# Softmax sums of pairs of key blocks: GpSimd adds the exponentials ahead of TensorE's ones matmuls, with four buffers of exponentials

## What is computed

```python
def _L0_attn_ref(x, q_w, k_w, v_w, q_b, k_b, v_b, out_w, out_b):
    ...
    attn = jnp.einsum('bhqd,bhkd->bhqk', q, k) * scaling
    probs = jax.nn.softmax(attn, axis=-1)
    out = jnp.einsum('bhqk,bhkd->bhqd', probs, v)
    out = out.transpose(0, 2, 1, 3).reshape(B, S, D)
    return out @ out_w.T + out_b
...
x = x + _L0_attn_ref(_layernorm(x, axis=-1), L0_attn_q_w, L0_attn_k_w, L0_attn_v_w, L0_attn_q_b, L0_attn_k_b, L0_attn_v_b, L0_attn_out_w, L0_attn_out_b)
```

## Time and profile before

| | |
|---|---|
| median of 3 runs | 1898.21 us (1896.54 to 1898.46) |
| the profiled execution | 1895.96 us |
| its span, first to last instruction | 1894.0 us, 28397 instructions |
| TensorE busy | 1565.4 us, 83% |
| VectorE busy | 1178.8 us, 62% |
| ScalarE busy | 864.6 us, 46% |
| GpSimd busy | 495.0 us, 26% |
| mean granted TensorE clock | 0.933 of full speed |

### The profile page before, as it was taken

The page is one execution under the profiler, slowest core; times in us unless marked ns, Lnnn a source line. Parts: engine busy times, 40 slices in busy tenths (PEclk is TensorE's granted clock), DMA queues, the critical chain, the costliest instruction groups (busy, mean ns, idle before and its releaser), DMA issues.

```text
span 1894.0 us, 28397 instructions
## 1 busy us (share of the span) xinstructions
PE 1565.4 (83%) x9300; PEld 608.4 (32%) x9301; DVE 1178.8 (62%) x1722; ACT 864.6 (46%) x1045; POOL 495.0 (26%) x417
## 2 busy tenths in 40 slices
PE   1899999999949863677779999999949999989827
PEld 1323323233226641333322323333223232323213
DVE  3664756647545535999756463646543676767678
ACT  1353352533523323777545445454635555463612
POOL 1503315033120014311131221212123141414117
PEclk9999999999979986888889999999979999999968
DMA  3700202102033445100031020202212020303002
GB/s 111 247 21 23 67 0 64 25 22 67 24 109 130 148 111 117 23 1 0 1 89 34 12 55 0 67 0 67 89 67 67 24 67 0 89 0 87 1 28 89
DMA packets 80844, 106.08 MB, mean 56 GB/s; under 512 B 14113, under 2 KB 51361, under 8 KB 80673
## 3 DMA queue, kind: packets, MB, share of 16 engines
q1 hardware_dynamic: 77216, 97.14, 17.3%
q0 software_dynamic: 3584, 8.39, 2.1%
HBM read 49.26 MB, written 18.35 MB: 36 GB/s over the span
## 4 chain that ended last, share of the span: by engine, by line
PE 59%; issue 15%; DVE 15%; ACT 4%; POOL 3%; DMA 2%; SPq 1%; DVEq 0%; POOLq 0%; ACTq 0%
PE ps L398 28%; PE ps L716 15%; PE ps L803 6%; PE ps L664 3%; PE ps L688 2%; ACT arena L914 2%; DVE arena L1630 1%; DVE xn L186 1%; PE ps L1517 1%; DVE arena L1098 1%; SPq L623 1%; DVE stats L175 1%; PE ps L737 1%; DVE arena L1641 1%; DVE arena L969 1%
## 5 line engine op out<-in xcount | busy, mean ns | idle before, releaser
L914 ACT ACTIVATE arena<-ps 128x1024 f32<-128x1024 f32 x384 | 372.1, 1024 | 175.9 <-PE ps L803 175.3
L716 PE MATMUL ps<-arena 128*32 128x512 f32 x3072 | 391.5, 616 | 32.8 <-DVE arena L969 24.0
L935 DVE TENSOR_REDUCE arena<-ps 128x2 f32<-128x1024 f32 x256 | 306.4, 1220 | 154.6 <-PE ps L664 154.5
L398 PE MATMUL ps<-xt,w 128*128 128x512 f16 (+1 forms) x1872 | 298.8, 312 | 32.6 <-DVE arena L1003 20.6
L803 PE MATMUL ps<-arena 97*128 97x512 f16 (+1 forms) x768 | 207.6, 383 | 9.7 <-ACT arena L914 6.0
L398 PEld LDWEIGHTS ps<-xt,w 128*128 128x128 f16 (+1 forms) x1872 | 155.0, 100 | 170.8 <-issue 67.1
L398 PE MATMUL ps<-w,arena 128*128 128x512 f16 (+1 forms) x804 | 178.7, 379 | 12.7 <-issue 12.7
L1204 POOL TENSOR_TENSOR arena<-arena 128x512 f16<-128x512 f32 x96 | 115.1, 1201 | 244.1 <-ACT arena L900 206.1
L896 ACT ACTIVATE arena<-ps,arena 128x512 f32<-128x512 f32 x96 | 65.8, 686 | 222.2 <-PE ps L398 179.4
L1115 POOL TENSOR_TENSOR arena<-arena 128x512 f32<-128x512 f32 x36 | 50.5, 1404 | 378.0 <-DVE arena L974 378.0
L1098 DVE TENSOR_SCALAR arena<-arena 128x1024 f32<-128x1024 f32 x128 | 106.7, 839 | 67.1 <-ACT arena L914 66.4
(11 more groups left out here) (176 smaller groups left out, 1909.8 us busy)
## 6 DMA issues: line engine op xcount, KB each, us to landing
arena<-arena SPq DMA_DIRECT2D x576, 64.0 KB, 2.0
raw<-in_ctxT SPq DMA_DIRECT2D x8, 1024.0 KB, 5.4
raw<-in_ffn_parts SPq DMA_DIRECT2D x16, 512.0 KB, 3.5
sorted_x<-arena SPq DMA_DIRECT2D x1, 4864.0 KB, 25.3
arena<-sorted_x SPq DMA_DIRECT2D x19, 256.0 KB, 3.5
sorted_y<-arena SPq DMA_DIRECT2D x19, 256.0 KB, 2.1
out<-x SPq DMA_DIRECT2D x16, 256.0 KB, 2.1
x<-in_x SPq DMA_DIRECT2D x1, 3072.0 KB, 13.8
```

The lines of the kernel that those rows point to most:

```text
L398: last = pe.matmul(out, left[l](cl[k]), right[r](cr[k]), start=start and k == 0 and a == 0, stop=stop and k == n - 1 and a == 2)
L716: last = pe.matmul(self.m.ps[HD * j:HD * (j + 1), 7 if ones else 6, :], left, self.pt[:, u % 2, j * S:(j + 1) * S], start=kb == 0, stop=kb ...
L914: act.activation(self.pt[:, u % 2, 2 * h * S:(2 * h + 2) * S], flat(self.m.ps[:, 2 * h:2 * h + 2, :]), ACT.Exp, scale=SOFTMAX_SCALE).then_ ...
L935: v.tensor_reduce(self.mx[:, g % 2, j:j + 2, t:t + 1].rearrange("p h t -> p (h t)"), self.slot_banks(item, b), AX.X, ALU.max).then_inc(sel ...
```

## The change

In the two self-attentions GpSimd adds the exponentials of two units, 2n and 2n+1, into one buffer, in four instructions of 128x512 (`pool_pair`). That is done for n = 0 to 6; TensorE then multiplies the sum of the pair by ones, instead of each unit, and units 14 and 15 are multiplied by ones as before. A group's two pairs are read by TensorE at the end of steps 4g+3 and 4g+5 (`sums_at`), those of group 3 in step 15 and behind it. There is one buffer for the pair's sum, so GpSimd waits until TensorE has read the pair before. There are four buffers of exponentials: the two of `pt` and the two of `raw`, in which weights lie while they are loaded; so the following phase's first weights are loaded only after the last sums.

VectorE inverts a group's sums one unit later, in step 4g+6, writes the inverse to bank 7 and does the multiplication that GpSimd did (`dve_context`). The norm is applied after unit 11 instead of 12. The values' matmuls no longer wait for the turn of the sums, in the cross-attention neither: there the ones matmuls do.

```diff
-        self.pt = take(2 * HG * S).rearrange("p (n t) -> p n t", n=2)
-        self.vb, self.vhigh = self.pt[:, 1, 0:D], self.pt[:, 1, D:2 * D].bitcast(F16)[:, 0:D]
+        pt = take(2 * HG * S).rearrange("p (n t) -> p n t", n=2)
+        self.vb, self.vhigh = pt[:, 1, 0:D], pt[:, 1, D:2 * D].bitcast(F16)[:, 0:D]
+        self.pts = [pt[:, 0], pt[:, 1]] if cross else [pt[:, 0], pt[:, 1], flat(m.raw[:, 0]), flat(m.raw[:, 1])]
+        if not cross:
+            self.pair_sum = turning if rope else flat(m.tails[1])
...
-        self.pv_done, self.ctx_free = s("pv_done", NB * NH), s("ctx_copied", NB * (C - 1))
+        self.values_done, self.unit_summed, self.ctx_free = s("values_done", NB * NH), s("unit_summed", NB * (NH if cross else 2)), s("ctx_copied", NB * (C - 1))
+        self.paired, self.pair_read = (s(name, 0 if cross else NB * self.ADDS * n) for name, n in (("pairs_added", HG), ("pair_sums_read", 1)))
...
         if self.rope:
+        if not self.cross:
+            sp.wait_ge(*self.at(self.unit_summed, NB * 2))
...
+    def pe_values(self, pe, u, b):
         g, kb = divmod(u, T)
-        if not ones:
-            for h in range(2):
-                pe.wait_ge(*self.at((self.clipped if self.cross else self.exp_done)[h], b * NH + u + 1))
-            if kb == 0 and g:
-                pe.wait_ge(*self.at(self.ctx_free, b * (C - 1) + g))
-                pe.wait_ge(*self.at(self.sums_read, b * C + g))
-            if u == 0:
-                pe.wait_ge(*self.at(self.normed, b * C))
-                if not self.cross:
-                    pe.wait_ge(*self.at(self.slot_free[1], self.slot_count(1, b + 1)))
+        for h in range(2):
+            pe.wait_ge(*self.at((self.clipped if self.cross else self.exp_done)[h], b * NH + u + 1))
+        if kb == 0 and g:
+            pe.wait_ge(*self.at(self.ctx_free, b * (C - 1) + g))
+        if u == 0:
+            pe.wait_ge(*self.at(self.normed, b * C))
+            if not self.cross:
+                pe.wait_ge(*self.at(self.slot_free[1], self.slot_count(1, b + 1)))
         for j in range(HG):
-            left = self.ones if ones else self.v[:, kb, HD * (HG * g + j):HD * (HG * g + j + 1)]
-            last = pe.matmul(self.m.ps[HD * j:HD * (j + 1), 7 if ones else 6, :], left,
-                             self.pt[:, u % 2, j * S:(j + 1) * S], start=kb == 0, stop=kb == T - 1,
-                             tile_position=(0, HD * j))
-        if ones:
-            last.then_inc(self.pv_done, 1)
+            last = pe.matmul(self.m.ps[HD * j:HD * (j + 1), 6, :], self.v[:, kb, HD * (HG * g + j):HD * (HG * g + j + 1)],
+                             self.p(u)[:, j * S:(j + 1) * S], start=kb == 0, stop=kb == T - 1, tile_position=(0, HD * j))
+        last.then_inc(self.values_done, 1)
+    def p(self, u):
+        return self.pts[u % len(self.pts)]
+    def sums_at(self, u):
+        if self.cross:
+            return [((u - 1) // T, ("unit", u - 1), u % T == 1, u % T == 0)] if u else []
+        found = []
+        if u < NH and u % T == T - 1:
+            found.append((u // T, ("pair", u // 2 - 1), True, False))
+        if u < NH and u > T and u % T == 1:
+            found.append((u // T - 1, ("pair", (u - T) // 2 + 1), False, True))
+        if u >= NH - 1:
+            found.append((C - 1, ("unit", u - 1), False, u == NH))
+        return found
+    def pe_sums(self, pe, u, b):
+        for g, (kind, n), first, done in self.sums_at(u):
+            if first and g:
+                pe.wait_ge(*self.at(self.sums_read if self.cross else self.normed, b * C + g))
+            if kind == "pair":
+                pe.wait_ge(*self.at(self.paired, HG * (b * self.ADDS + n + 1)))
+            p = self.pair_sum if kind == "pair" else self.p(n)
+            for j in range(HG):
+                last = pe.matmul(self.m.ps[HD * j:HD * (j + 1), 7, :], self.ones, p[:, j * S:(j + 1) * S],
+                                 start=first, stop=done, tile_position=(0, HD * j))
+            if kind == "pair":
+                last.then_inc(self.pair_read, 1)
+            else:
+                last.then_inc(self.unit_summed, 1)
     def pe_proj(self, pe, n, b):
         m = self.m
...
             if u:
-                self.pe_values(pe, u - 1, b, ones=False)
+                self.pe_values(pe, u - 1, b)
             self.pe_planned(pe, b, u, 3)
-            if u:
-                self.pe_values(pe, u - 1, b, ones=True)
+            self.pe_sums(pe, u, b)
         for i in range(T):
             self.wait_read(pe, ("v", i), b)
...
             for u in range(NH):
                 g, kb = divmod(u, T)
                 for h in range(2):
                     act.wait_ge(*self.at(self.st_full[h], b * NH + u + 1))
-                    act.wait_ge(*self.at(self.pv_done, b * NH + max(u - 1, 0)))
-                    act.activation(self.pt[:, u % 2, 2 * h * S:(2 * h + 2) * S], flat(self.m.ps[:, 2 * h:2 * h + 2, :]),
+                    before = u - len(self.pts)
+                    act.wait_ge(*self.at(self.values_done, b * NH + max(before + 1, 0)))
+                    if self.cross:
+                        act.wait_ge(*self.at(self.unit_summed, b * NH + max(before + 1, 0)))
+                    elif before >= 0:
+                        act.wait_ge(*self.at(self.paired, HG * (b * self.ADDS + before // 2 + 1)))
+                    act.activation(self.p(u)[:, 2 * h * S:(2 * h + 2) * S], flat(self.m.ps[:, 2 * h:2 * h + 2, :]),
...
-    def dve_invert(self, v, g, b):
-        v.wait_ge(*self.at(self.pv_done, b * NH + T * (g + 1)))
+    def dve_invert(self, v, g, b, out=None):
+        if self.cross:
+            v.wait_ge(*self.at(self.unit_summed, b * NH + T * (g + 1)))
+        elif g < C - 1:
+            v.wait_ge(*self.at(self.pair_read, b * self.ADDS + 2 * g + 2))
+        else:
+            v.wait_ge(*self.at(self.unit_summed, b * 2 + 2))
         v.wait_ge(*self.at(self.normed, b * C + g))
         v.transpose(self.sums, self.m.ps[:, 7, :]).then_inc(self.sums_read, 1)
         v.wait_ge(*self.at(self.sums_read, b * C + g + 1))
         one = self.inverse.rearrange("p (n k) -> p n k", k=1)
         v.reciprocal(one, blocked(self.sums)[:, :, 0:1]).then_inc(self.reciprocals, 1)
         v.wait_ge(*self.at(self.reciprocals, b * C + g + 1))
-        v.transpose(blocked(self.sums), one.broadcast_to([P, NQ, HD])).then_inc(self.inverted, 1)
+        v.transpose(blocked(self.sums if out is None else out), one.broadcast_to([P, NQ, HD])).then_inc(self.inverted, 1)
+    def dve_context(self, v, g, b):
+        v.wait_ge(*self.at(self.inverted, b * C + g + 1))
+        v.wait_ge(*self.at(self.ctx_free, b * (C - 1) + g + 1))
+        v.tensor_tensor(self.ctxn, self.ctxn, self.m.ps[:, 7, :], ALU.mult).then_inc(self.normed, 1)
...
-            if g and kb == 1:
-                self.dve_invert(v, g - 1, b)
+            if g and kb == (1 if self.cross else 2):
+                self.dve_invert(v, g - 1, b, None if self.cross else m.ps[:, 7, :])
+                if not self.cross:
+                    self.dve_context(v, g - 1, b)
...
-            if u == 12 and not self.cross:
+            if u == 11 and not self.cross:
                 if self.rope:
...
+        self.pool_context_low(g, c, b)
+
+    def pool_context_low(self, g, c, b):
         g.wait_ge(*self.at(self.ch, b * C + c + 1))
         g.tensor_tensor(self.ct[:, 1, c, :], self.ctxn, self.ct[:, 0, c, :], ALU.subtract).then_inc(self.cl, 1)
+
+    def pool_pair(self, g, n, b):
+        for h in range(2):
+            g.wait_ge(*self.at(self.exp_done[h], b * NH + 2 * n + 2))
+        if n == 0:
+            g.wait_ge(*self.at(self.fl, (b + 1) * self.NPROJ))
+        g.wait_ge(*self.at(self.pair_read, b * self.ADDS + n))
+        for j in range(HG):
+            cols = slice(j * S, (j + 1) * S)
+            g.tensor_tensor(self.pair_sum[:, cols], self.p(2 * n)[:, cols], self.p(2 * n + 1)[:, cols], ALU.add).then_inc(self.paired, 1)
...
-        for c in range(C - 1):
-            if c == C - 2:
+        for n in range(self.ADDS):
+            if n == self.ADDS - 2:
                 self.norm.pool(g, b)
-            self.pool_context(g, c, b)
+            self.pool_pair(g, n, b)
+            if n > 1 and n % 2 == 0:
+                self.pool_context_low(g, n // 2 - 1, b)
```

18 lines of the change are left out of this document (11 added, 7 removed).

## The result

| | before | after |
|---|---|---|
| median of three runs | 1898.21 us | 1928.08 us (1924.8 to 1936.2) |
| profiled execution | 1895.96 us | 1936.2 us (span 1934.4) |
| after / before | | 1.017, 95% interval 1.013 to 1.021 |

What follows compares the result with a forecast made beforehand. TensorE, busy 83%, was taken as the bound, VectorE's reductions pacing steps with p's. attn1 +12.8, attn0 +13.6, clock +5.6 and xattn -3.7 gave +28.3 on 1895.96, 1924.3; forecast 1925, range 1898 to 1942.

Steps and rivals of the forecast that it cites:

- All four signs: Idle before pair 3/4 products; norm instructions 1.4 us; step 6's second p waits; output projection 21.7 us after unit 11.
- Tail and norm: Unit 11 to output projection: norm meets pair 5's additions, x 5.8 us after the power; about +2.6 us a batch.
- rival 3: More falls of the clock, from waits at step 6, pair 3, unit 12's scores and x: 1936; chance 0.13.
- Front: First exponentials to unit 11's: unit 11 starts 0.6 us later a batch in attn1, 0.8 in attn0.
- The walk: Step-by-step timeline of attn1 batch 2 and attn0 batch 1, from the first exponentials to unit 11.
- the second p of step 6: In attn1 batch 2 it waits behind the inversion until t = 22.75, where before it stood at 21.2.
- GpSimd's loop: Additions, product and crossings: 6.3 us for two units, against 5.64 in steps without p, 6.6 to 6.9 mid-batch.
- 1.2 us of waiting at pair 3: In attn1 batch 2 TensorE reaches pair 3 at t = 31.3; GpSimd's additions end at 32.4.
- Rival 1: GpSimd stays hidden, the inversion fits ahead of the reductions and the middle runs at 6.3 us: 1883; chance 0.14.
- The clock: One fall to the lower clock per attn0 batch behind the wait for x, 1.4 us each; none in attn1.
- Cross-attention: Step 13's values no longer wait for the sums; VectorE's clipping is the next wait: -0.9 us a batch.
- The turn of the sums in step 13: In the self-attentions it no longer holds the values (1.54 us), but lies ahead of the same wait: no gain.

Runs made afterwards that it cites:

- e6_small_adds: The changed kernel with each GpSimd addition over 8 of its 512 columns, a pair's ones matmul reading its first block: 1897.0 us.
- e7_half_reductions: The changed kernel with each VectorE reduction of the maxima over 256 of its 512 columns per bank: 1894.7 us.
- e8: The changed kernel with both additions of 8 columns and reductions over half their columns: 1850.0 us.
- e10_three: The changed kernel with moments and power earlier, inversion and context behind the step's last reduction, and two pair-sum buffers in the attention without rotation: 1900.4 us.
- e1_split: The kernel before with only the wait for the turn of the sums moved from values to ones matmuls, separate semaphores, no pairs: 1870.2 us.
- e9_before_half_reductions: The kernel before with each reduction of the maxima over 256 of its 512 columns per bank: 1886.7 us, against 1895.8 beside it.

## Why the prediction held, and where it did not

**Outcome.** Right in sign and size: 1928.1 for 1925, inside the range. All four signs that it named for being right are in the rows. But its steps fared unevenly, and that the sum came so near is in part luck: the fronts lost 17.2 us in the profiled execution where it had 5.6, the cross-attention gave 9.1 where it had 3.7.

**Tail and norm: right, with a second wait beside it in `attn1`.** x 5.9 us behind the power (forecast 5.8), tails +2.6 and +4.05 with the clock (2.6 and 4.0). In `attn0` e6_small_adds shows it by removal: without additions beside the norm the tail falls by 5.4 us. In `attn1` it falls by 0.5 us only: there the maxima's DMA ahead of unit 12, with the fall of the clock that came behind it, costs nearly as much once x is no longer late. The sum left that wait out (rival 3 names the scores of unit 12). It did no harm to the forecast, since x was awaited behind it.

**Front: the mechanism was one of two, and the other was larger.** The walk had the p's and the second p of step 6 in it (forecast t = 22.75, measured 1272.06 - 1249.94 = 22.1), but the text put the loss on GpSimd's loop, "nearly the pace of before in the middle", and expected 1.2 us of waiting at pair 3, where the row has 0.47. For the two batches that it walked through it gave +0.6 and +0.8, where +0.8 (`attn1` batch 2) and +4.5 (`attn0` batch 1) were measured. The fronts of e6 and e7 show what holds them: of 320.5 us in after, e6_small_adds takes away 10.9 and e7_half_reductions 36.7. The loop is one limit there, VectorE's reductions are the larger one. The loop's sizes (4.97 us of additions, 6.2 us from pair 3's start at 1277.60 to pair 4's at 1283.80) were right to 0.1 us. What was missed is a sentence: the ones matmuls were what TensorE did while VectorE reduced. The prediction saw that "steps with two p's ... hold idle time already" and used it only for steps 1 and 2. Rival 1, with GpSimd hidden and the inversion fitting in, was priced at 1883; e6_small_adds, where the additions are as good as gone and the reductions stay, is at 1897.0.

**The clock: right in kind, far too small.** Forecast 5.6 us, only behind the wait for x in `attn0`. The matmuls of after take 40 us more in the eight heads than the same matmuls in e8, whose clock is 0.97 to 1.00 against 0.87 to 0.97. Falls came in steps 1 to 4 of `attn0` too, behind waits of 1.14 and 1.33 us, and in `attn1` behind 1.74. One of them:

```profile
225.01 0.28 PE L688 MATMUL ps<-ident,arena 128*16 128x128 f32 x1 [1.14 <-DVE arena L978]
...
226.22 1.94 PE L723 MATMUL ps<-arena 128*32 128x512 f32 x8
```

The row that could have told this was there: in the kernel before the same step showed a fall in three of four batches. In after step 1 fell in three batches again, and steps 2 and 3 now with it. What that costs can be read in e10_three: steps 2 and 3 last 4.0 and 3.7 us in its batch of 60.2 us, 5.4 and 5.3 in those of 63.5.

**Cross-attention: mis-sized.** -0.9 forecast per batch, -2.3 measured. The next wait is the clipping, as the prediction said, 1.40 us long. What it left out is that the shorter wait also spares the fall of the clock (3.40 us for a row that takes 1.92 at full clock).

**The turn of the sums in step 13 "gives nothing" in the self-attentions.** So in after, where x is awaited right behind it. Without pairs it gives 1.6 to 1.7 us a batch (e1_split).

**Not foreseen, and not the change's: the end.** Behind the last heads, in code that is the same, the profiled run of after lost 5.9 us. VectorE's four int32 instructions there (1.42 us for four at that place before) met GpSimd's:

```profile
1910.16 5.46 DVE L1886 TENSOR_SCALAR arena<-arena 128x512 int32<-128x512 int32 x4
1915.55 1.42 DVE L1889 TENSOR_SCALAR arena<-arena 128x512 f32<-128x512 f32 x4
```

The stretch behind the last heads is 93.4 to 93.7 us long in seven of the fourteen profiled runs and 98.9 to 99.6 in the other seven, e9_before_half_reductions among these, which has no pairs. So this is no loss of the change but a matter of the single execution; it may be half of why the runs of after differ by 11 us. What decides between the two lengths was not tested.

**Open.** Why some batches of the same kernel fall to the lower clock and others do not (e10_three: 60.2 and 63.5 us) was not settled. No run moves the moments or the last scaling alone, so how much the maxima's DMA costs in `attn1` is read from rows only. And no run separates what is lost to the order of the inversion in `attn0` from the clock there.

## What to carry to other kernels

A matmul that is taken off TensorE may have been the cover of another engine's work: before pricing it, list what TensorE waits for right behind it, and price the saving only down to that engine's pace, 1.86 us per reduction here, and add what the lower clock costs behind the new waits. When work moves off an engine, move the plan of what stands beside it too: respacing the p's gave 25 us, as much as the best of the other repairs. And take a change apart by its own parts first: the one wait that was moved was worth 29 us, and the rest had hidden it. Last, when a run takes one cause away and the time hardly moves in some stretch, look for the wait that stood second there, as in the tails of `attn1`.

## What the runs showed of the hardware

- **Idle time on TensorE has a price of its own.** Behind many waits of 1.14 to 2.6 us the next rows ran at the lower clock, 1.2 GHz (1.94 us for eight records of 512 columns instead of 1.06); with 0.80 us left of a wait they did not, and behind 1.54 us in the kernel before they did not either.
- **GpSimd's additions stretch some VectorE instructions and not others.** Beside GpSimd's additions, tensor_scalar from SBUF to SBUF takes 1.4 us each, in float32 (L186, beside a pair's) instead of 0.48 and in int32 (L1886, beside those to x at the end) instead of 0.36. The reductions from PSUM stay at 1.22 to 1.23 beside them, and four bn_stats on SBUF take what they take in e6_small_adds, where GpSimd is idle (2.46). In after, beside pair 4 (1283.80 to 1288.77):

```profile
1286.25 2.46 DVE L175 BATCH_NORM_STATS2 stats<-x 128x6 f32 x4
```

  The Trainium skill ("SBUF — State Buffer", section "Who interferes with whom") says that a VectorE instruction with at most one input in SBUF, outside the two-port modes, does not contend with GpSimd. The trace agrees, with 2.46 us for the four bn_stats and 1.22 to 1.23 for a reduction.
- **A GpSimd addition is nearly all length.** Four of 8 columns take 0.69 us, four of 512 take 4.95.
